# Row norms of three weight matrices: one ScalarE square and one VectorE sum each, replaced by four ScalarE squares that accumulate

## What is computed

```python
def step(carry, inp):
    w0_, w1_, w2_ = carry
    qi, ki, vi, lr0i, lr1i, lr2i = inp
    gate = ki @ w0_
    hb = ki @ w2_
    ...
    w1g = newtonschulz5(jnp.einsum('bch,bcd->bhd', hidden * lr1i, vi))
    w0g = newtonschulz5(jnp.einsum('bcd,bch->bdh', ki * lr0i, dgba))
    w2g = newtonschulz5(jnp.einsum('bcd,bch->bdh', ki * lr2i, dhbm))
    w1_ = w1_ + w1g
    w0_ = w0_ + w0g
    w2_ = w2_ + w2g
    w0_ = w0_ / (jnp.linalg.norm(w0_, axis=1, keepdims=True) + 1e-05) * w0n
    ...
    oi = silu(qi @ w0_) * (qi @ w2_) @ w1_
    return ((w0_, w1_, w2_), oi)
```

## Time and profile before

| what | value |
|---|---|
| runs of the kernel | 1853.25, 1862.06, 1863.24 us |
| median | 1862.06 us |
| the profiled execution, its own time | 1872.18 us |
| its span, first to last instruction | 1870.4 us |
| mean granted TensorE clock | 0.938 |
| fast-weight phase, halves counted at the power of line 1397 | 32, from 202.9 to 944.5 us |
| TensorE, VectorE, ScalarE, GpSimd busy | 86%, 63%, 47%, 42% of the span |

### The profile page before, as it was taken

How to read it: one execution, slowest core, us unless ns; L and a number is a source line. 1 busy time by engine, 2 the same in 40 slices (tenths; PEclk the granted TensorE clock), 3 DMA queues, 4 the chain that set the end, 5 groups by cost and what they waited for, 6 DMA issues and landing times. The chain is left out here.

```text
span 1870.4 us, 41123 instructions
## 1 busy us (share of the span) xinstructions
PE 1605.9 (86%) x11163; PEld 1197.3 (64%) x11227; DVE 1176.2 (63%) x4255; ACT 884.2 (47%) x2156; POOL 783.5 (42%) x818
## 2 busy tenths in 40 slices
PE   3993799888888888898872499999999999998996
PEld 1662577666666676666651377777777777776764
DVE  2662578878887778888873454444444444443877
ACT  1773377656566666666650133333333333332221
POOL 0331233455455545555567133333333333342333
PEclk7996799989998989999995699999999999999999
DMA  2675444444444442223223455555555556323997
GB/s 87 186 213 170 118 138 129 129 146 141 128 139 136 146 129 81 78 82 95 67 80 120 128 161 160 166 160 167 159 157 167 153 166 202 95 57 74 266 269 191
DMA packets 264288, 263.54 MB, mean 141 GB/s; under 512 B 87931, under 2 KB 235880, under 8 KB 264080
## 3 DMA queue, kind: packets, MB, share of 16 engines
q1 hardware_dynamic: 200592, 170.98, 32.1%
q0 software_dynamic: 21504, 51.18, 7.7%
q10 hardware_dynamic: 41984, 38.82, 7.6%
HBM read 141.91 MB, written 127.31 MB: 144 GB/s over the span
## 5 line engine op out<-in xcount | busy, mean ns | idle before, releaser
L1728 POOL DMA_INDIRECT scratch_y<-e_eo,e_goes x256 | 250.4, 978 | 408.8 <-ACT e_eo L1818 349.4
L1754 PE MATMUL e_psGU<-wgu,e_xT 128*128 x1024 | 352.1, 466 | 4.9 <-ACT e_xT L1811 2.7
L1862 DVE COPY e_hT<-e_psH 88x256 f32<-88x256 f32 x256 | 107.7, 421 | 338.3 <-PE e_psH L1763 257.5
L1770 PE MATMUL e_psD<-wd,e_hT 88*128 x1024 | 263.8, 380 | 0.0
L1754 PEld LDWEIGHTS e_psGU<-wgu,e_xT 128*128 128x128 f32 x1024 | 183.8, 190 | 92.6 <-issue 24.9
L1392 POOL DMA_INDIRECT scratch_buf<-rows,dest x192 | 192.0, 1000 | 49.1 <-issue 48.9
L1402 POOL TENSOR_TENSOR f_wnr<-f_wss,f_half 128x4 f32<-128x4 f32 x96 | 99.8, 1040 | 266.9 <-DVE f_wss L1212 265.0
L1807 ACT ACTIVATE e_sgm<-e_psGU 128x176 f32<-128x176 f32 x256 | 81.2, 317 | 239.5 <-PE e_psGU L1754 200.7
L1770 PEld LDWEIGHTS e_psD<-wd,e_hT 88*128 88x128 f32 x1024 | 174.1, 190 | 14.1 <-issue 0.4
L1818 ACT ACTIVATE e_eo<-e_psD 128x256 f32<-128x256 f32 x256 | 98.1, 383 | 159.0 <-issue 93.3
L1740 PEld LDWEIGHTS e_psX<-ident,e_xg 128*128 128x128 f32 x512 | 72.3, 141 | 73.1 <-issue 39.6
(11 more groups left out here) (305 smaller groups left out, 3779.3 us busy)
## 6 DMA issues: line engine op xcount, KB each, us to landing
e_xg<-scratch_buf ACTq DMA_DIRECT2D x256, 132.0 KB
scratch_y<-f_blank SPq DMA_DIRECT2D x64, 384.0 KB
c_g<-scratch_y SPq DMA_DIRECT2D x64, 384.0 KB, 12.0
scratch_qkvT<-q_tT SPq DMA_DIRECT2D x16, 768.0 KB
wgu<-in_wgT SPq DMA_DIRECT2D x64, 176.0 KB
wgu<-in_wuT SPq DMA_DIRECT2D x64, 176.0 KB
wd<-in_wdT SPq DMA_DIRECT2D x64, 176.0 KB
scratch_buf<-f_blank SPq DMA_DIRECT2D x65, 132.0 KB, 2.2
```

Of the source, the lines that this page charges most:

```text
L1728: pool.indirect_dma_start(out=T["y"], out_offset=bass.IndirectOffsetOnAxis(goes[:, n:n + 1], 0), in_=eo[:, n % OB, :], in_offset=None, bou ...
L1754: mm = pe.matmul(psGU[:, j % 2, 0:2 * F], xT[:, j % 2, k, :], wgu[:, bass.ds(buf, 1), k, :].rearrange("p b n -> p (b n)"), start=(k == 0), ...
L1770: mm = pe.matmul(psD[:, j % 2, 0:D], hT[0:FH, j % 2, k, :], wd[0:FH, buf, k, :].rearrange("p b n -> p (b n)"), start=(k == 0), stop=(k == 1))
L1862: v.tensor_copy(hT[0:FH, b, :, :].rearrange("p k t -> p (k t)"), psH[0:FH, b, 0:2 * P]).then_inc(htd, 1)
```

## The change

`square` issues four activations, one for each block of 128 columns, each with `accum_out`, so that ScalarE itself writes the row's sum of squares to `f_wss`. The function `row_norms` and its six entries in `DVE_ORDER` are gone. `row_root` on GpSimd waits for the four increments of `square` instead of the one of `row_norms`. All other entries of all tables stay in their order.

```diff
@@ DVE_ORDER (one of six entries that go)
-    ("row_norms", 1, 1, 0), ("update", 1, 1, 1), ("squares", 0, 0, 0), ("gate_x", 0, 2, 0), ("squares", 0, 0, 1),
...
+    ("update", 1, 1, 1), ("squares", 0, 0, 0), ("gate_x", 0, 2, 0), ("squares", 0, 0, 1),
@@ semaphores
-        a2p, a2d, b2p, b2d, t3p, wud, wsqd, wssd, wn1 = (sig(n, LOTS) for n in (
-            "a2p", "a2", "b2p", "b2", "t3p", "wu", "wsq", "wss", "wn1"))
+        a2p, a2d, b2p, b2d, t3p, wud, wn1 = (sig(n, LOTS) for n in (
+            "a2p", "a2", "b2p", "b2", "t3p", "wu", "wn1"))
+        wssd = sig("wss", Q * LOTS)
@@ ScalarE
             def square(x, it, m):
                 act.wait_ge(wud[x].sem, wud[x].at(it, m + 1))
-                act.activation(flat(wsq[:, x, m, :, :]), flat(WT[:, m, x, :, :]), ACT.Square).then_inc(wsqd[x].sem, 1)
+                for q in range(Q):
+                    act.activation(wsq[:, x, m, q, :], WT[:, m, x, q, :], ACT.Square,
+                                   accum_out=wss[:, x, m * Q + q:m * Q + q + 1]).then_inc(wssd[x].sem, 1)
@@ VectorE
-            def row_norms(x, it, m):
-                v.wait_ge(wsqd[x].sem, wsqd[x].at(it, m + 1))
-                v.tensor_reduce(wss[:, x, m * Q:(m + 1) * Q], wsq[:, x, m, :, :], AX_X, ALU.add).then_inc(wssd[x].sem, 1)
@@ GpSimd
             def row_root(x, it, m):
                 cols = slice(m * Q, (m + 1) * Q)
-                pool.wait_ge(wssd[x].sem, wssd[x].at(it, m + 1))
+                pool.wait_ge(wssd[x].sem, wssd[x].at(it, Q * (m + 1)))
```

More of the change, by code:

```diff
@@ L522 @@
     ("renorm", 0, 1, 1), ("norm_x", 1, 3), ("norms", 1, 1), ("a", 1, 1, 0), ("a", 1, 1, 1), ("a", 1, 1, 2),
-    ("b", 1, 1, 0), ("b", 1, 1, 1), ("row_norms", 0, 1, 2), ("b", 1, 1, 2), ("read", 1, 2, 0), ("place", 1, 4),
+    ("b", 1, 1, 0), ("b", 1, 1, 1), ("b", 1, 1, 2), ("read", 1, 2, 0), ("place", 1, 4),
     ("factors", 0, 1, 2), ("gate", 0, 0), ("slope", 0, 0), ("slope_2", 0, 0), ("both", 0, 0), ("token_dg", 0, 0),
     ("rows_x", 1, 3), ("token_dhb", 0, 0), ("update", 1, 1, 0), ("token_hid", 0, 0), ("o_eps", 1, 2),
-    ("row_norms", 1, 1, 0), ("update", 1, 1, 1), ("squares", 0, 0, 0), ("gate_x", 0, 2, 0), ("squares", 0, 0, 1),
-    ("factors", 1, 1, 0), ("squares", 0, 0, 2), ("row_norms", 1, 1, 1), ("row_sums", 0, 0), ("renorm", 1, 1, 0),
+    ("update", 1, 1, 1), ("squares", 0, 0, 0), ("gate_x", 0, 2, 0), ("squares", 0, 0, 1),
+    ("factors", 1, 1, 0), ("squares", 0, 0, 2), ("row_sums", 0, 0), ("renorm", 1, 1, 0),
     ("totals", 0, 0), ("update", 1, 1, 2), ("pick", 0, 3), ("factors", 1, 1, 1), ("renorm", 1, 1, 1),
     ("norm_x", 0, 2), ("norms", 0, 0), ("a", 0, 0, 0), ("a", 0, 0, 1), ("a", 0, 0, 2), ("b", 0, 0, 0),
-    ("b", 0, 0, 1), ("row_norms", 1, 1, 2), ("b", 0, 0, 2), ("read", 0, 1, 0), ("place", 0, 3), ("factors", 1, 1, 2),
+    ("b", 0, 0, 1), ("b", 0, 0, 2), ("read", 0, 1, 0), ("place", 0, 3), ("factors", 1, 1, 2),
     ("gate", 1, 0), ("slope", 1, 0), ("slope_2", 1, 0), ("both", 1, 0), ("token_dg", 1, 0), ("rows_x", 0, 2),
-    ("token_dhb", 1, 0), ("update", 0, 0, 0), ("token_hid", 1, 0), ("o_eps", 0, 1), ("row_norms", 0, 0, 0),
-    ("update", 0, 0, 1), ("squares", 1, 0, 0), ("gate_x", 1, 2, 0), ("squares", 1, 0, 1), ("factors", 0, 0, 0),
-    ("squares", 1, 0, 2), ("row_norms", 0, 0, 1), ("row_sums", 1, 0), ("renorm", 0, 0, 0), ("totals", 1, 0),
+    ("token_dhb", 1, 0), ("update", 0, 0, 0), ("token_hid", 1, 0), ("o_eps", 0, 1), ("update", 0, 0, 1), ("squares", 1, 0, 0), ("gate_x", 1, 2, 0), ("squares", 1, 0, 1), ("factors", 0, 0, 0),
+    ("squares", 1, 0, 2), ("row_sums", 1, 0), ("renorm", 0, 0, 0), ("totals", 1, 0),
     ("update", 0, 0, 2), ("pick", 1, 3), ("factors", 0, 0, 1),
@@ L1327, in _ @@
                 "token_dg": token_dg, "token_dhb": token_dhb, "token_hid": token_hid, "squares": squares, "row_sums": row_sums, "totals": totals,
-                "norms": norms, "a": scale_a, "b": scale_b, "update": update, "row_norms": row_norms,
+                "norms": norms, "a": scale_a, "b": scale_b, "update": update,
                 "factors": factors, "renorm": renorm, "read": read})
```

## The result

| what | before | after |
|---|---|---|
| median of four runs | 1862.65 us | 1923.88 us |
| lowest and highest | 1853.25, 1867.43 | 1921.73, 1932.7 |
| profiled execution, own time and span | 1872.18, 1870.4 | 1921.73, 1920.0 |
| mean granted TensorE clock | 0.938 | 0.911 |

The ratio is 1.0345, 95% interval 1.0314 to 1.0376: 61 us slower, where 18.5 was forecast. The direction was right, the time lies 26 us above the range.

What follows compares the result with a forecast made beforehand. The prediction took each half as a chain through in-order queues, with VectorE not the bound from `scale_a` to the next update. Terms 19.0 + 11.5 - 12.0 gave +18.5 us, 1880.5 for the median; range 1862 to 1898.

Steps and rivals of the forecast that it cites:

- Part I: Stretch of each half from the first update to `scale_a`; forecast to grow by 19.0 and 11.5 us.
- 19.0 for the second square: Lot 1's square, ahead of the XT evictions, delays totals and cast: 0.63 in 32 halves, less 0.10 in 12.
- 11.5 for the first: Lot 0's square, ahead of `f_Wn` and X, delays X where these follow without a gap: 11.5 us in all.
- The price of 0.63 a square: ScalarE's queue: four accumulated squares cost 1.17 us against 0.54 for one of 512 columns, so +0.63 each.
- cheap end of +0.28: ScalarE's square by the skill's activation costs, accumulator read unpriced: 0.80 us against 0.52, so +0.28 each.
- VectorE's freed sums: 96 sums leave VectorE, 58 us of its queue; the question was whether anything waits for VectorE behind them.
- The rival in which VectorE is the bound: VectorE's lifted sums shorten update to `scale_a`: 1847 us, at most down to 1804; chance of faster 0.07.
- so all of part I's end moves: +0.63 in each: Behind the totals' cast VectorE runs without a gap, so the second square's delay reaches `scale_a` in 32 halves.
- one rival at 0.05: Dearer accumulated squares on ScalarE (+1.43 each, near 1920 us) or a lower granted TensorE clock; chance 0.05 together.
- the -12.0: End of part II: GpSimd's sends come 0.6 us earlier, so the update waiting for "remote" does too, in 20 halves.
- The first rival: Sends give nothing back, the lag before the update being TensorE's own: +30.5, or 1892.5 us; chance 0.22.

Runs made afterwards that it cites:

- the single lots: Kernel before with only one lot's square accumulated: lot 1 (second square) 1866.21 us, ratio 1.0195; lot 0 (first) 1841.09, 1.0076; lot 2 (third) 1830.24, 1.0009.
- the tails with and without sends: Kernel before with the sends of two tiles put together, twelve in every second half and none in the others: 1960.53 us, ratio 1.0461.

## Why the prediction was wrong

**Part I: right in place; in size right for one kind of half, and the sum partly by luck.** Forecast 19.0 for the second square and 11.5 for the first, 30.5 in all; measured +30.3 on the chip of the forecast. In the halves where X started 1.74 after the update, and no fall of the clock reached part I, it mostly went from 11.04 to 12.24: +1.20 against 1.16 forecast. Where X had started at 1.89 to 2.08 it grew by 0.86 to 0.88 in four halves and by 0.2 in two, and where it had started at 2.2 to 2.8 mostly by 0.2 to 0.9, since the changed kernel's X starts at 2.39 in most of these. The forecast gave every half 0.63 for the second square alone, so there it was too high. What made the sum come out is four halves with part I at 13.55 to 15.07, 8.9 us over the usual 12.24. In them X starts 2.81 to 4.97 after the update, and ScalarE has waited 2.3 to 3.7 us for "remote" around the update, as ahead of the half from 641.01:

```profile
640.88 0.60 ACT L1016 ACTIVATE f_B<-prod 128x512 bf16<-128x512 f32 x1 [3.62 <-remote]
```

No term of the forecast has that. On a chip without such waits the change adds 23.5 to part I, and the single lots 17.6 and 7.0; there the kernel before starts X 1.89 after the update and so hides more of the first square. The price of 0.63 a square, taken from the sibling instruction, stands: 1.18 against 0.54. The Trainium skill, page "ScalarE: Activation LUTs", section "What ACT_TABLE_LOAD costs", would have made a square of 128 columns 0.20 us of queue; the rows of the changed kernel say 0.29, as the forecast took it. Its cheap end of +0.28 is out.

**VectorE's freed sums: right for part I.** They became most of the wait for the totals, 23.1 us. The rival in which VectorE is the bound, and the kernel gets faster, is refuted: the kernel got slower, and the freed sums are worth 0.8 us in part I and 6 by the medians. So is, for this kernel, what the prediction made of the Trainium skill, page "Perfetto Trace Analysis", section "Identifying the Most-Contended Engine": VectorE was at 86.61% and ScalarE at 67.97%, and moving work from the first to the second cost 2.1 to 3.45%. The section calls occupancy a fair measure of how close VectorE, ScalarE and GpSimd are to roofline; that it is a fair guide for moving work between them, as the prediction has it, is not in it.

**What failed first: the term that was not there.** The step "so all of part I's end moves: +0.63 in each" priced ScalarE's delay as a delay and no more. The same delay opens gaps on TensorE, and its granted clock answers with 1.2 GHz over the following microseconds. Measured: from 58 to 140 us at the low level, +14.6 us in the stretch to `x2` on the first chip, +13.4 on another; 8.9 us of this stretch came back when the gaps were filled. The forecast held this as half of one rival at 0.05 and had no price for it. The trace of before could have given one: in five of its halves the clock falls and `x2` comes 1.4 to 2.5 late, and I read its mean clock of 0.938 as a constant.

**What failed second: the -12.0.** "0.6 in each of the 20 halves if it belongs to the sends. I take the second." `renorm` and the sends did come 0.6 earlier, exactly as forecast: the last send starts 11.03 after `scale_a`, 11.62 before the change. Timeline of after, GpSimd and VectorE, in two neighbouring halves:

```profile
692.33 1.14 POOL L1390 DMA_INDIRECT scratch_buf<-rows,dest  x1 [0.30 <-issue]
...
706.44 1.89 DVE L1201 TENSOR_TENSOR f_A<-prod,f_r 128x512 bf16<-128x512 f32 x3
...
712.42 1.03 POOL L1405 TENSOR_TENSOR f_WT<-f_WT,f_wsc 128x512 f32<-128x512 f32 x1 [3.72 <-DVE f_wsc L1220]
...
717.47 1.15 POOL L1390 DMA_INDIRECT scratch_buf<-rows,dest  x1 [0.31 <-issue]
718.66 0.69 DVE L1210 TENSOR_TENSOR f_WT<-prod,f_WT 128x512 f32<-128x512 f32 x1 [0.35 <-remote]
```

The update at 694.21 (shown above, with the result) trails its last send by 1.88, the one at 718.66 by 1.19. The tails of the 24 halves with sends fall into three kinds (us):

| halves, mean tail, start of the update after that of the last send | long | middle | short |
|---|---|---|---|
| before | 13 halves, 10.54, 1.93 to 2.44 | 7 halves, 8.98, 0.37 to 0.52 | 4 halves, 8.35, ahead of it |
| after | 19 halves, 9.85, 1.84 to 2.51 | 5 halves, 9.07, 1.18 to 1.20 | none |

So the long tails did get shorter, by 0.69 in the mean, and the distance that I had found held in them. But there are more of them. In before, 11 of the 24 updates started before the last send did, or at most 0.52 after; with the sends 0.6 earlier every update starts at least 1.18 after it and waits. Half by half, the 13 that were long before lost 10.2 us together and the other eleven gained 9.5, which leaves the -0.9 of the tail. On two chips of the experiments it looks the same: before has 15 long, 6 middle and 3 short tails, the change 20 long ones of 9.87 in the mean and 4 middle ones. The step that failed is that each half keeps its kind of wait. This is read from the rows of two executions of each kernel; no run moves the sends alone on a chip with these waits. The first rival's time, 1892.5, has the right sum for the tail, but its reason, a lag that is TensorE's own and hangs on no send, is refuted by the tails with and without sends.

**What is left.** Part I, the stretch to `x2` and the tail make 44.0 of the 49.6 between the two profiled executions; 5.6 lie outside the 30 halves and were not looked into. The other 11.6 up to 61.2 are the distances of the profiled executions to their medians.

**What stays open.** How a send holds up signals between other engines, and why only on some chips: the waits showed in the first result and on two chips of the experiments (the first result's chip may be one of these), and not on two others, where the same kernel is some 36 us faster with a tail shorter by 38 (24 halves by 1.6). The ratio also differs, 1.021 to 1.024 without the waits against 1.0326 and 1.0345 with them; 7 us of that is part I, the rest was not separated. Also why ScalarE's "remote" waits make X late in 4 to 8 halves of some executions. And whether VectorE's freed sums are worth anything: 6 us by the medians, up to 11 by the intervals.

## What to carry to other kernels

A delay on an engine that feeds TensorE can cost twice: once as itself, and again if it cuts TensorE's work into pieces with gaps, because the matmuls after the gaps may be granted half the clock. Before costing such a delay at its length, look in the trace for places where the clock has already fallen, read what the engine did just before, and ask how near the other repeats are to it. Moving the delaying instruction behind the evictions that TensorE waits for gave back 34 us; matmuls that nobody needs gave back 8.9 us in the stretch that the clock had made longer, and 24 us in the medians.

An engine at 87% busy gave little or nothing when it was relieved, because in a chain of in-order queues it was waited for almost nowhere that its relief reached; and naming the right cause of a wait is not enough for a credit. In this kernel the earlier sends shortened the long waits and made halves wait that had hardly waited before: count both. And a sum that comes out right is no proof of its terms; compare it half by half.

## What the runs showed of the hardware

In the changed kernel gaps of 0.2 to 0.9 us, 1.0 to 1.8 us together, were followed by a granted clock of 0.50 for 3.4 or 6.8 us at a time, in 23 to 28 halves of 30. In the kernel before, with one gap of 0.42 to 0.62 at the same place, it fell in 2 to 8 halves. How much idle time there is does not decide it alone: in the half of before from 647.86 TensorE idles 0.40 ahead of `turn` and 0.62 ahead of `row_sums`, and the clock stays at 2.4 GHz. With ten matmuls added it fell in 8 halves of the changed kernel in place of 25, and in 1 of before in place of 2. The Trainium skill, page "TensorE: Matmul & The Clock Gate", section "HAM oscillation — how this bites in real kernels", takes half of the time at the low clock as lost; by that, the 85 us more at 1.2 GHz of the changed kernel, on the chip with a run of before at 17, would be an estimated 43 us. Measured were 13.4 in the stretch to `x2`. At full clock TensorE idles 0.97 before the second `back`, for VectorE's `renorm`; in a half with the fall that idle is 0.29, so part of the slow matmuls ran in time that was idle anyway. The rows, before and the change on that chip:

```profile
646.32 0.66 PE L936 MATMUL prod<-ident,f_WT 128*128 128x128 f32 x4 [0.97 <-DVE f_WT L1227]
```

```profile
647.79 1.11 PE L936 MATMUL prod<-ident,f_WT 128*128 128x128 f32 x4 [0.29 <-DVE f_WT L1225]
```

With GpSimd's indirect DMAs in the tail, other engines waited for signals that the profile calls "remote": 1.6 us a half in the mean, and up to 5.1 when eight follow each other. It showed in the first result and on two chips of the experiments, and not on two others with the same kernel.

One accumulated square of 128 columns costs ScalarE's queue 0.29 us, its accumulator read of 0.19 included; four are 1.18 against 0.54 for one square of 512 columns.
